# Transposed rows held in banks by token halves, and the next pass's first gate and up tile computed by token halves

## The reference

```python
def ffn(x, gate_w, up_w, down_w, gate_scale, up_scale, down_scale):
    # weights are rounded to float8_e4m3 first; gate_w, up_w 256x768, down_w 768x256
    gate = silu((x @ gate_w) * gate_scale)
    up = (x @ up_w) * up_scale
    return ((gate * up) @ down_w) * down_scale

x = x + attention(layernorm(x))        # causal, one head, with its own norm and residual
x = x + ffn(layernorm(x))
x = x + s4d(layernorm(x))              # a convolution by FFT along an axis, plus x * D
x = x + ffn(layernorm(x))
```

## Time and profile before

| | us |
|---|---|
| median of 3 runs | 127.24 |
| lowest and highest | 127.01, 127.3 |
| profiled execution | 127.35 |
| its span in the trace | 125.6 |
| TensorE busy in it | 116.5 (93%) |
| VectorE busy | 94.4 (75%) |
| GpSimd busy | 86.8 (69%) |
| ScalarE busy | 77.6 (62%) |

### The profile page before, as it was taken

One profiled execution on the slowest core, in us unless ns is written; L12 is line 12 of the kernel. 1 busy time (PEld: TensorE's weight loads), 2 busy tenths in 40 slices (PEclk: granted clock), 3 DMA queues, 4 the chain that ended last, 5 costly groups with the idle time before them and its releaser, 6 DMA issues.

```text
span 125.6 us, 2089 instructions
## 1 busy us (share of the span) xinstructions
PE 116.5 (93%) x666; PEld 77.3 (62%) x666; DVE 94.4 (75%) x226; ACT 77.6 (62%) x147; POOL 86.8 (69%) x168
## 2 busy tenths in 40 slices
PE   5997999999999999999999999989999869999970
PEld 5885468658668758745769545567446457556640
DVE  0398999919865866949797899947899946784592
ACT  2145079695875468858865278865578764579800
POOL 2246469999999888888433578889978870038831
PEclk9999999999999999999999999999999999999999
DMA  3998940000000000000000000000000000000404
GB/s 90 297 277 322 354 135 8 0 0 0 0 0 0 5 5 0 0 0 0 0 0 5 0 0 0 0 3 5 0 0 0 3 0 0 5 0 24 143 0 167
DMA packets 5682, 5.80 MB, mean 46 GB/s; under 512 B 1140, under 2 KB 5160, under 8 KB 5672
## 3 DMA queue, kind: packets, MB, share of 16 engines
q1 hardware_dynamic: 4648, 5.52, 13.3%
q10 hardware_dynamic: 960, 0.15, 0.7%
q0 software_dynamic: 64, 0.02, 0.1%
HBM read 4.63 MB, written 1.05 MB: 45 GB/s over the span
## 4 chain that ended last, share of the span: by engine, by line
PE 66%; DVE 11%; POOL 10%; ACT 4%; issue 3%; DMA 3%; SPq 0%; POOLq 0%; DVEq 0%; ACTq 0%
PE psum L1195 22%; PE psum L1211 10%; PE psum L1134 7%; PE psum L1109 7%; PE psum L1074 6%; POOL rstd L296 4%; DMA qkv_sb<-in_qkv 3%; PE psum L1067 3%; DVE stats L696 3%; PE psum L1156 2%; PE psum L1122 2%; POOL f_tail L451 2%; ACT h_rows L559 2%; ACT normed L529 2%; PE psum L1050 2%
## 5 line engine op out<-in xcount | busy, mean ns | idle before, releaser
L607 ACT ACTIVATE gated<-psum,scales 128x512 f32<-128x512 f32 x24 | 16.3, 681 | 13.1 <-PE psum L1195 13.1
L451 POOL TENSOR_TENSOR f_tail<-fused,f_head 128x512 f16<-128x512 f32 x12 | 14.1, 1173 | 12.8 <-ACT f_head L613 12.5
L1211 PE MATMUL psum<-down,f_head 128*128 128x256 bf16 x96 | 22.1, 273 | 0.5 <-POOL f_tail L451 0.5
L1211 PE MATMUL psum<-down,f_tail 128*128 128x256 bf16 x96 | 22.0, 272 | 0.0
L958 DVE SCALAR_TENSOR_TENSOR fused<-psum,up_scales_fit,gated 128x512 f32<-128x512 f32 (+1 forms) x25 | 17.8, 716 | 4.6 <-PE psum L1195 3.3
L613 ACT ACTIVATE f_head<-fused 128x512 f16<-128x512 f32 (+1 forms) x25 | 15.1, 606 | 3.4 <-DVE fused L958 3.2
L966 DVE TENSOR_TENSOR f_tail<-fused,f_head 128x512 f16<-128x512 f32 (+1 forms) x13 | 9.7, 749 | 9.2 <-ACT f_head L613 9.1
L1195 PE MATMUL psum<-h_head,up 128*128 128x512 f16 x48 | 14.3, 379 | 0.0
L1195 PE MATMUL psum<-h_tail,up 128*128 128x512 f16 x48 | 14.3, 379 | 0.0
L1195 PE MATMUL psum<-h_tail,gate 128*128 128x512 f16 x48 | 14.3, 379 | 0.0
L1195 PE MATMUL psum<-h_head,gate 128*128 128x512 f16 x48 | 14.3, 379 | 0.0
(11 more groups left out here) (167 smaller groups left out, 257.2 us busy)
## 6 DMA issues: line engine op xcount, KB each, us to landing
x_in<-in_x SPq DMA_DIRECT2D x4, 256.0 KB, 4.2
qkv_sb<-in_qkv SPq DMA_DIRECT2D x3, 256.0 KB, 4.0
gate_raw<-in_gate_w SPq DMA_DIRECT2D x1, 768.0 KB, 6.8
up_raw<-in_up_w SPq DMA_DIRECT2D x1, 768.0 KB, 8.6
down_raw<-in_down_w SPq DMA_DIRECT2D x1, 768.0 KB, 10.3
out<-x_in SPq DMA_DIRECT2D x3, 256.0 KB, 2.1
wo_sb<-in_o_proj SPq DMA_DIRECT2D x1, 256.0 KB, 5.3
down_scale_all<-in_down_scale SPq DMA_DIRECT2D x1, 128.0 KB, 10.1
```

The lines of the kernel that those rows point to most:

```text
L451: pool.tensor_tensor(f_tail[:, m, :], fused[:, m % FUSED, :], f_head[:, m, :], ALU.subtract).then_inc(f_tail_by_pool, 1)
L607: act.activation(gated[:, m % 2, :], psum[:, BANK_GATE[m % 2], :], ACT.Silu, scale=gate_scales[:, m:m + 1]).then_inc(gated_ready, 1)
L1211: last = pe.matmul(down_columns(n, t), part[:, m, t * P:t * P + P], down16[:, m, :], start=(m == 0 and (t % 2 == 0 or n == 2 * B - 1) and ...
```

## The change

Three things change. First, the transposes of half `half` go to bank `BANK_H[half]`, both chunks side by side, so that a bank holds all channels of 256 tokens. `copy_h` and `h_tails` take a half instead of a chunk: still one instruction of 128x512 elements, with a view of 2 pieces of 256. Second, the copy and the subtraction of half 0 move from the next pass's start to this pass's end. Third, for the tiles in `HALVED` (none in pass 0, tile 0 in passes 1 and 2, tiles 0 and 1 in pass 3) the gate and up products are made by token halves, 8 matmuls of 256 columns each: half 0 behind `down(n, 3)` and in front of `turn_h(n + 1, 1)`, half 1 in the tile's old place. A half does the gate and the up products with `h_head` first, then both with `h_tail`.

```diff
-            def copy_h(n):
-                for c in range(C):
-                    act.wait_ge(h_turned, C * n + c + 1)
-                    act.activation(h_head[:, c, :], psum[:, BANK_H[c], :], ACT.Copy).then_inc(h_head_ready, 1)
+            def copy_h(n, half):
+                act.wait_ge(h_turned, 2 * n + half + 1)
+                act.activation(h_head[:, :, HALVES[half]], psum[:, BANK_H[half], :].rearrange("p (c s) -> p c s", c=C),
+                               ACT.Copy).then_inc(h_head_ready, 1)
...
                 if n >= 1:
-                    copy_h(n)
+                    copy_h(n, 1)
                 gate(n, 0)
...
                 gate(n, 5)
                 head(n, 4)
+                if n < 3:
+                    copy_h(n + 1, 0)
                 if n in (1, 2):
                     normalise(3, tiles[2], x3)
                     normalise(3, tiles[3], x3)
...
-            def h_tails(n):
-                for c in range(C):
-                    dve.wait_ge(h_head_ready, C * n + c + 1)
-                    dve.tensor_tensor(h_tail[:, c, :], psum[:, BANK_H[c], :], h_head[:, c, :],
-                                      ALU.subtract).then_inc(h_tail_ready, 1)
+            def h_tails(n, half):
+                dve.wait_ge(h_head_ready, 2 * n + half + 1)
+                dve.tensor_tensor(h_tail[:, :, HALVES[half]], psum[:, BANK_H[half], :].rearrange("p (c s) -> p c s", c=C),
+                                  h_head[:, :, HALVES[half]], ALU.subtract).then_inc(h_tail_ready, 1)
...
                     tail(n, 3)
                     fuse(n, 5)
+                    h_tails(n + 1, 0)
                     tail(n, 5)
...
+                    if n == 0 and m == M - 1:
+                        h_tails(1, 0)
...
                 if not first:
-                    pe.wait_ge(h_tail_ready, n * C)
+                    pe.wait_ge(h_tail_ready, 2 * (n - 1) + half + 1)
                 for c in range(C):
                     for t in (2 * half, 2 * half + 1):
-                        last = pe.transpose(column(BANK_H[c], t * P, P), h_rows[:, t, c * P:c * P + P], ident[:])
-                    if half == 1:
-                        last.then_inc(h_turned, 1)
+                        last = pe.transpose(column(BANK_H[half], c * S // 2 + t % 2 * P, P), h_rows[:, t, c * P:c * P + P], ident[:])
+                last.then_inc(h_turned, 1)
...
+            def gate_up_half(n, m, half):
+                cols = HALVES[half]
+                if half == 0:
+                    pe.wait_ge(gated_ready, (n - 1) * M + (m + 5))
+                    pe.wait_ge(fused_ready, (n - 1) * M + (m + 5))
+                for part, ready in ((h_head, h_head_ready), (h_tail, h_tail_ready)):
+                    pe.wait_ge(ready, 2 * n + (half + 1))
+                    for w, banks, made in ((gate16, BANK_GATE, gate_made), (up16, BANK_UP, up_made)):
+                        for c in range(C):
+                            last = pe.matmul(column(banks[m % 2], cols.start, S // 2), w[:, c, m * P:m * P + P],
+                                             part[:, c, cols], start=(part is h_head and c == 0),
+                                             stop=(part is h_tail and c == C - 1), skip_group_check=True)
+                        if half == 1 and part is h_tail:
+                            last.then_inc(made, 1)
...
+            HALVED = [(), (0,), (0,), (0, 1)]
...
                 for m in range(M):
-                    gate_up(n, m)
+                    if m in HALVED[n]:
+                        gate_up_half(n, m, 1)
+                    else:
+                        gate_up(n, m)
...
                 turn_h(n + 1, 0)
                 down(n, M - 3)
+                for m in HALVED[n + 1]:
+                    gate_up_half(n + 1, m, 0)
                 turn_h(n + 1, 1)
                 down(n, M - 2)
                 down(n, M - 1)
```

More of the change, by code:

```diff
@@ L600, in _ @@
             copy_probs(K - 1)
-            copy_h(0)
+            copy_h(0, 0)
+            copy_h(0, 1)
             act.activation(silu_table[:], params[:, 0:1], ACT.Silu)
@@ L908, in _ @@
             attention_out(K - 2)
-            h_tails(0)
+            h_tails(0, 0)
+            h_tails(0, 1)
             attention_out(K - 1)
@@ L970, in _ @@
                 if n >= 1:
-                    h_tails(n)
+                    h_tails(n, 1)
                 if n == 3:
@@ L1192, in gate_up @@
                         for c in range(C):
-                            if m == 0 and w is gate16:
-                                pe.wait_ge(ready, n * C + (c + 1))
+                            if m == 0 and w is gate16 and c == 0:
+                                pe.wait_ge(ready, 2 * n + 2)
                             last = pe.matmul(column(banks[m % 2], 0, S), w[:, c, m * P:m * P + P], part[:, c, :],
```

## The result

| | us |
|---|---|
| before, median of 4 runs | 127.16 |
| changed, median of 4 runs | 128.33 (128.19 to 128.66) |
| ratio | 1.009, 95% interval 1.0053 to 1.0127 |
| profiled execution of the changed kernel | 128.19, span 126.4 |

Slower by 0.9%, 1.2 us (forecast: slower, 128.0, range 127.1 to 128.7).

The account below looks back on a forecast made before the run. Bound: TensorE's waits for h_rows end long chains, GpSimd's in pass 1, GpSimd's then VectorE's in pass 2. Delay 0.70 + 0.07 = 0.77, plus 0.03 behind: 127.35 + 0.80 = 128.15 profiled, 128.0 median; range 127.1 to 128.7.

Parts of the forecast that it names:

- No gap at pass 1, so the work there only delays: Change from pass 0 to 1: half tile stands before the downs, filling no gap; GpSimd's chain starts 0.78 us late.
- Two branches, SiLU's later start and the late downs: Pass 1: SiLU makes fused(1, 0) 0.76 us late, downs make scaled_down and residual 0.78 late; both feed the statistics.
- GpSimd's chain passes the delay on unchanged: Pass 1, from var_eps to the second rows' release: back to back, so the 0.78 us delay stays 0.78.
- The gap at pass 2 is filled and eaten: Change from pass 1 to 2: second turn_h 0.94 us late with 0.87 of pass 2 done, net 0.07 lost.
- The gap at pass 3 wins a little: Change from pass 2 to 3: second turn_h 1.60 us late with 1.74 done, 0.14 won there.
- fused(3, 1) binds tile 3: Pass 3: after VectorE's 3.69 us stretch fused(3, 1) ends at 112.42; TensorE waits 0.86 before tile 3's up products.
- The new forms cost like the plain ones, half-width matmuls 0.109: Split-view copy 0.594 us and subtraction 0.680 as plain; 256-column matmuls 0.109, the split adding under 0.03 a tile.
- C: Rival: split view costs like two half-width instructions, 0.22 us more a copy, 0.49 a subtraction; about 129.5; chance 0.03.
- D: Rival: the 64 half-width matmuls do not keep 0.109 us; at 0.13 they add 1.3, giving 129; chance 0.02.
- A: Rival: gaps are filled, faster, chiefly 1.74 us at the third change; 126.4 with no delay d; chance 0.14.
- B: Rival, no change: delay into pass 1 stays hidden but fused(3, 1) binds; 0.07 us, 127.3; chance 0.13.
- The end: End of the kernel: 0.80 us later, 128.15 on the profiled execution's scale, 128.0 forecast for the median.

Follow-up runs that it names:

- e3: The changed kernel with half tiles in pass 1 only (none in passes 2 and 3): 128.08 us, ratio 1.0076 to the kernel before.
- e2: The changed kernel with no half tile in pass 1, those in passes 2 and 3 kept: 127.22 us, ratio 1.0022 to the kernel before.
- e9: The changed kernel with only tile 0 of pass 1 halved, both halves in its old place behind the downs: 127.87 us, ratio 1.0060 to before.
- e5: The changed kernel with half 1 of a halved tile making all gate products before its up products: 128.05 us, ratio 1.0066 to before.
- e4: The changed kernel with void_beyond's four VectorE operations and its one-column product moved from pass 3 to pass 2: 127.34 us, ratio 1.0012 to before.
- e8: The changed kernel with no half tile in pass 1 and void_beyond with its product moved to pass 2: 126.33 us, ratio 0.9933 to before.
- e7: The changed kernel with no half tiles at all and void_beyond with its product moved to pass 2: 127.21 us, ratio 0.9998 to before.
- e11: The changed kernel with VectorE's f_tail of tile 0 in pass 1 moved in front of fused of tile 2: 128.18 us, ratio 1.0078 to before.

## Why the prediction was right, point by point

- **No gap at pass 1, so the work there only delays.** Right in direction and size at the statistics: var_eps 0.72 late, 0.78 forecast; e3 shows that this fill alone costs 0.97 us, e2 that without it the loss is gone.
- **Two branches, SiLU's later start and the late downs.** Half right. Both were late as worked out (0.73 and 0.69), but only fused(1, 0) bound: e9 has no late downs and still loses 0.8 of the 0.97 us. The residual had 0.28 us to spare, the wait of var_eps in the earlier trace rows, which the working passed over, so late downs alone would have made it about 0.4 late and not 0.78. It was luck that the other term had the same size (0.76): the forecast of the delay came out without settling which of the two ends last.
- **GpSimd's chain passes the delay on unchanged.** Wrong in size: 0.72 went in and 0.96 came out. This is the term that was mis-sized: "GpSimd's chain from 73.43 starts 0.78 late. From there it is back to back". It is back to back, but its operations are not of fixed length: they moved against VectorE's f_tail, and two took 0.61 + 0.88 us instead of 0.19 + 1.07. The missing 0.2 us is here. e9, e3 and e5 show it too: 0.45 in and 0.69 out, 0.73 in and 0.98 out, 0.51 in and 0.90 out.
- **The gap at pass 2 is filled and eaten.** Right: 1.11 late with 0.87 done (forecast 0.94). The delay there fell to 0.94 at the first turn for pass 3 instead of the 0.70 that I carried, the same 0.2 us further on.
- **The gap at pass 3 wins a little.** Forecast 1.60 late with 1.74 done, 0.14 won; measured 1.85, so 0.11 was lost. The difference is the delay of 0.94 instead of 0.70 that came in. e2 gives the part without the delay, 0.90, which is the formula's.
- **fused(3, 1) binds tile 3.** Right: the stretch of 3.69 is unchanged, tile 3's up products could have started at 111.19 + 0.43 = 111.62 and started 0.85 later, 0.86 forecast, and e4 takes it away, and with it the loss.
- **The new forms cost like the plain ones, half-width matmuls 0.109.** Right; rivals C and D fall. A falls because both of its conditions failed: d was 0.94, and fused(3, 1) bound. e8 gives them both and lands at 126.33, where A put 126.4. B falls with the delay of pass 1; e2 is its case, 127.22 for its 127.3.
- **The end.** 0.80 forecast, 0.98 in the trace, 1.17 between the medians. The two profiled executions differ by 0.84 only (127.35 and 128.19): the one before lay 0.19 above its median, and the changed kernel's was the fastest of four. 0.2 of the missing 0.37 us is the stretch on GpSimd; the other 0.2, between trace and medians, has no cause that the runs show.

## What to carry to other kernels

In this kernel, work put into a gap was won only where what hangs on the delayed work behind it has slack, and where no other engine holds up the next consumer. Both can be checked by subtraction in the trace, and one fill of three passed, that of pass 3, once void_beyond had moved. When a tile's products are cut in two by tokens, its first output is complete later even if the sum of the work is the same, and an activation that ran beside the rest of the tile moves onto the path. Before filling a gap at the end of a chain, look for the fixed stretch on the next engine (here four small operations and four scalings between two fused) and move what can go elsewhere first: alone it won nothing (e7), with the fills 0.9 us (e2 to e8).

## What the runs showed of the hardware

GpSimd's small operations of 2 columns (var_eps, mean_rstd, std, neg_mean_rstd) take 0.19 us. Beside a VectorE operation with two inputs from SBUF (f_tail) they took up to 0.77 and ended some 0.05 us behind it: mean_rstd 76.13 to 76.74 beside f_tail 76.01 to 76.69, and, in e11, std 75.40 to 76.06 beside f_tail 75.33 to 76.01. Beside fused, which has one of its two inputs in PSUM, the power rstd kept its 0.70 us (74.58, beside fused at 74.72). It works in the other direction too: in the changed kernel VectorE's f_tail at 81.79 took 1.28 us instead of the 0.68 of the one at 76.01, beside GpSimd's own f_tail from 81.36 to 82.52. The Trainium skill (SBUF — State Buffer, Summary: rules for kernel authors) states this: where a VectorE instruction has two SBUF inputs and the GpSimd instruction reads SBUF, the second to issue waits until the first ends. The traces agree, with one limit: the longest, mean_rstd of 0.77 at 93.88 and that of 0.76 in e5, began 0.04 and 0.02 us in front of f_tail by the profile's stamps and were held all the same, so who issued first cannot be read from starts that lie so close.

What follows for a chain of such small operations is that its length changes with its phase against the other engine: from var_eps to the next turn it took 9.25 us before, 9.49 in the changed kernel and in e9, and 9.64 in e5. A shift of 0.5 us in became 0.7 us out in e9, and 0.9 in e5.
